# Node passes that hold loaded and stored tiles twice and load a turn ahead

## What is computed

```python
h = jnp.maximum(_layernorm(x, axis=-1), 0.0)
x = x + _L0_gnn_ref(h, edge_attr_8, ...)            # message passing, product with W_upd
h = jnp.maximum(_layernorm(x, axis=-1), 0.0)
x = x + _L1_gnn_ref(h, edge_index, edge_attr_8, ...) # convolution by edge attributes
h = jnp.maximum(_layernorm(x, axis=-1), 0.0)
x = x + _L2_gnn_ref(h, edge_attr_8, src, dst, ...)   # encoder, 2 rounds of edge and node MLP, decoder
h = jnp.maximum(_layernorm(x, axis=-1), 0.0)
x = x + _L3_gnn_ref(h, edge_index, edge_weight, ...) # 2 GCN convolutions
```

## Time and profile before

| | before |
|---|---|
| median of 3 runs | 24420.91 us (24419.03 to 24428.73) |
| profiled execution | 24420.0 us |
| its span | 24418.2 us |
| busy PE, DVE, ACT, POOL | 78%, 55%, 25%, 23% of the span |
| node passes: first reduction to last store, n0 to n6 | 160, 367, 347, 329, 348, 91, 73 us |
| one turn's compute, n0 to n6 | 19.4, 59.4, 60.7, 53.2 to 54.5, 58.1 to 59.6, 11.8, 6.3 us |

### The profile page before, as it was taken

The page is one execution under the profiler, slowest core; times in us unless marked ns, Lnnn a source line. Parts: engine busy times, 40 slices in busy tenths (PEclk is TensorE's granted clock), DMA queues, the critical chain, the costliest instruction groups (busy, mean ns, idle before and its releaser), DMA issues. The chain is left out here.

```text
span 24418.2 us, 718381 instructions
## 1 busy us (share of the span) xinstructions
PE 18952.0 (78%) x285234; PEld 16845.7 (69%) x285234; DVE 13480.2 (55%) x32301; ACT 6107.4 (25%) x12086; POOL 5619.6 (23%) x3991
## 2 busy tenths in 40 slices
PE   0566666666569996799999999959999999769797
PEld 0555555555549996678777778747777777668797
DVE  1777777777644444444444444444444444456565
ACT  0111111111112221344444444422222222211111
POOL 0788888888700000000000000000000000001010
PEclk9655555555557776899999999979999999855555
DMA  2222222222212221233333333324444444334444
GB/s 83 45 50 48 49 48 49 51 49 48 47 55 88 90 88 56 87 101 100 100 100 100 100 100 100 100 65 128 130 129 128 130 129 129 100 95 151 120 153 129
DMA packets 1485401, 2230.06 MB, mean 91 GB/s; under 512 B 773860, under 2 KB 961010, under 8 KB 1440840
## 3 DMA queue, kind: packets, MB, share of 16 engines
q1 hardware_dynamic: 1168296, 1839.20, 24.1%
q10 hardware_dynamic: 176604, 300.32, 3.3%
q0 software_dynamic: 139040, 67.50, 2.9%
HBM read 1651.47 MB, written 551.16 MB: 90 GB/s over the span
## 5 line engine op out<-in xcount | busy, mean ns | idle before, releaser
L751 POOL DMA_INDIRECT records<-e_sort_rec,e_sort_index x3300 | 4775.9, 1447 | 1063.5 <-issue 1058.0
L2193 PE MATMUL e_s_ps_g<-e_s_parts,e_s_pick 128*128 128x64 bf16 x65340 | 3040.3, 203 | 717.5 <-DVE e_s_to_hot L1877 303.2
L2193 PEld LDWEIGHTS e_s_ps_g<-e_s_parts,e_s_pick 128*128 128x128 bf16 x65340 | 2777.4, 105 | 860.6 <-issue 374.5
L2286 POOL DMA_INDIRECT e_s_spill<-send,e_s_lists x220 | 212.8, 967 | 11482.2 <-DVE e_s_g_sb L1897 5895.5
L1893 DVE COPY e_s_g_sb<-e_s_ps_g 128x512 f32<-128x512 f32 x880 | 607.4, 690 | 2656.4 <-PE e_s_ps_h L2216 1251.2
L1317 PE MATMUL e_s_g<-e_s_parts,e_s_pick 128*128 128x16 bf16 x65340 | 1782.9, 174 | 319.6 <-DVE e_s_values L1233 219.8
L2198 PE MATMUL e_s_ps_g<-e_s_window,e_s_to_hot 128*128 128x64 bf16 x23100 | 2015.9, 202 | 3.7 <-issue 3.7
L1317 PEld LDWEIGHTS e_s_g<-e_s_parts,e_s_pick 128*128 128x128 bf16 x65340 | 1761.7, 104 | 348.5 <-DVE e_s_values L1233 240.3
L2240 PE MATMUL e_s_ps_sum<-e_s_unit,e_s_wide 128*128 128x128 f32 (+1 forms) x15400 | 1914.8, 276 | 5.3 <-DVE e_s_merged L1957 5.2
L1074 PE MATMUL e_sort_acc<-e_sort_thirds,e_sort_hot 128*128 128x48 f32 x7260 | 1574.6, 414 | 364.0 <-DVE e_sort_hot L912 364.0
L1074 PEld LDWEIGHTS e_sort_acc<-e_sort_thirds,e_sort_hot 128*128 128x128 f32 x7260 | 1557.0, 332 | 396.4 <-DVE e_sort_hot L912 396.4
(11 more groups left out here) (481 smaller groups left out, 33848.1 us busy)
## 6 DMA issues: line engine op xcount, KB each, us to landing
e_s_rows<-rows_d SPq DMA_DIRECT2D x330, 1088.0 KB, 5.3
e_s_hot<-hots_d SPq DMA_DIRECT2D x550, 560.0 KB, 3.6
e_s_states<-states SPq DMA_DIRECT2D x880, 256.0 KB, 4.2
e_s_to_rows<-rows_d SPq DMA_DIRECT2D x220, 608.0 KB, 6.1
e_s_rows<-rows_d SPq DMA_DIRECT2D x220, 544.0 KB, 4.9
e_s_rows<-rows_d SPq DMA_DIRECT2D x220, 512.0 KB, 3.9
e_s_to_rows<-rows_d SPq DMA_DIRECT2D x220, 512.0 KB, 4.9
states<-e_s_first_t ACTq DMA_DIRECT2D x440, 256.0 KB, 2.1
```

The source lines that it names most:

```text
L751: pool.indirect_dma_start(records, bass.IndirectOffsetOnAxis(ap=index[x][:, t:t + 1], axis=0), rec[x][:, t, :], None,).then_inc(written[x] ...
L2193: pe.matmul(to_, pick[p][:, h, here], parts[:, SPAN * c + h, r, :], start=h == 0 and r == 0, stop=False)
```

## The change

Tiles that are loaded or stored, and the table tile, are allocated twice; turn i uses the copy of its parity (`bigs[i % 2]`, `turns[i % 2]`). The other tiles stay single. SP issues the loads and the tables of turn i+1 ahead of the stores of turn i. Before load(i) with i at least 2 it waits for the end of the chains of turn i-2 and for the stores up to turn i-2, and for every i above 0 it waits until the loads of turn i-1 have landed. Since the loads no longer wait for the end of the turn before, DVE does: before turn i it waits for the end of all five chains of turn i-1. The memset clears both table tiles, and SP waits for both. The five turns are written out on all engines in place of one and a loop, so counts and addresses are constants, and the increments of `sp_tick` are gone. The bodies of the steps are the same; they take the tiles as an argument.

```diff
@@ node_pass @@
             if step == steps[0]:
-                return node_loaded, i * (16 * n_loads) + (b_loaded + 16 * n_loads)
+                return node_loaded, (i + 1) * (16 * n_loads) + b_loaded
...
-                sp.wait_ge(tables_cleared[name], 1)
+                sp.wait_ge(tables_cleared[name], 2)
...
-                    sp.dma_start(big["tab"][:, :, k, :], node_rows(agg[k])[bass.ds(i, 1)].squeeze(0)).then_inc(node_loaded, 16)
+                    sp.dma_start(bigs[i % 2]["tab"][:, :, k, :], node_rows(agg[k])[i]).then_inc(node_loaded, 16)
...
-                load_tables(0)
-
-            def body(i, first, last=False):
-                if not first:
+            def load(i):
+                if i >= 2:
                     for u in range(K):
-                        sp.wait_ge(q[u].sem, q[u].end(i - 1))
-                        sp.sem_inc(sp_tick, 1)
-                    sp.wait_ge(node_stored, i * (16 * len(stores)) + b_stored)
-                    sp.sem_inc(sp_tick, 1)
+                        sp.wait_ge(q[u].sem, q[u].end(i - 2))
+                    sp.wait_ge(node_stored, (i - 1) * (16 * len(stores)) + b_stored)
+                if i:
+                    sp.wait_ge(node_loaded, i * (16 * n_loads) + b_loaded)
                 for tile, rows_ in loads:
-                    sp.dma_start(tile, node_rows(rows_)[bass.ds(i, 1)].squeeze(0)).then_inc(node_loaded, 16)
-                if tables is not None and not last:
-                    for u in range(K):
-                        sp.wait_ge(q[u].sem, q[u].at("agg_sum", i))
-                        sp.sem_inc(sp_tick, 1)
-                    load_tables(i + 1)
+                    sp.dma_start(by_unit(bigs[i % 2][tile]), node_rows(rows_)[i]).then_inc(node_loaded, 16)
+                if tables is not None:
+                    load_tables(i)
+
+            load(0)
+            for i in range(NODE_TURNS):
+                if i + 1 < NODE_TURNS:
+                    load(i + 1)
                 for rows_, tile, step in stores:
                     for u in range(K):
                         sp.wait_ge(q[u].sem, q[u].at(step, i))
-                        sp.sem_inc(sp_tick, 1)
-                    sp.dma_start(node_rows(rows_)[bass.ds(i, 1)].squeeze(0), by_unit(big[tile])).then_inc(node_stored, 16)
-
-            body(0, True)
-            with sp.Fori(1, NODE_TURNS - 1) as i:
-                body(i, False)
-            body(NODE_TURNS - 1, False, True)
+                    sp.dma_start(node_rows(rows_)[i], by_unit(bigs[i % 2][tile])).then_inc(node_stored, 16)
             sp.wait_ge(node_stored, b_stored + 16 * len(stores) * NODE_TURNS)
...
-                dve.memset(big["tab"][:, :, :, :], 0.0).then_inc(tables_cleared[name], 1)
-            rolled(dve, NODE_TURNS, lambda i, first: dve_body(dve, q, ready, i))
+                for x in range(2):
+                    dve.memset(bigs[x]["tab"][:, :, :, :], 0.0).then_inc(tables_cleared[name], 1)
+            for i in range(NODE_TURNS):
+                if i:
+                    for u in range(K):
+                        dve.wait_ge(q[u].sem, q[u].end(i - 1))
+                dve_body(dve, q, ready, i, t=turns[i % 2])
...
-                rolled(act, NODE_TURNS, lambda i, first: act_body(act, q, ready, i))
+                for i in range(NODE_TURNS):
+                    act_body(act, q, ready, i, t=turns[i % 2])
...
-                rolled(pe, NODE_TURNS, lambda i, first: pe_body(pe, q, ready, i))
+                for i in range(NODE_TURNS):
+                    pe_body(pe, q, ready, i, t=turns[i % 2])
@@ pass_scope @@
-    def pass_scope(name, tiles):
+    def pass_scope(name, tiles, twice):
...
-        big = {k: sb(f"{name}_{k}", [shape[0], K] + shape[1:], F32, st) for k, shape in tiles.items()}
-        t = {k: [tile[:, u] for u in range(K)] for k, tile in big.items()}
+        big = [{k: sb(f"{name}_{k}", [shape[0], K] + shape[1:], F32, st) for k, shape in tiles.items()}]
+        big.append({k: sb(f"{name}_{k}_odd", [shape[0], K] + shape[1:], F32, st) if k in twice else big[0][k] for k, shape in tiles.items()})
+        t = [{k: [tile[:, u] for u in range(K)] for k, tile in big[x].items()} for x in range(2)]
```

More of the change, by code:

```diff
@@ L2727, in edge_pass, with node_pass @@
             advance(scattered[t], 16 * UNITS)
-    def node_pass(name, loads, tables, stores, steps, dve_body, act_body, pe_body, bufs, big):
+    def node_pass(name, loads, tables, stores, steps, dve_body, act_body, pe_body, bufs, bigs, turns):
         q = [Chain(node_chain[u], base(node_chain[u]), steps) for u in range(K)]
@@ L2919, in _gnn, with n0_dve, n0_act @@
     st, t, ps, big = pass_scope("n0", dict(x=[P, C, F], c=[P, C, F], sq=[P, C, F], v=[P, 3, 8], h=[P, C, F], ht=[TW, P],
-                                      y=[P, 512]))
+                                      y=[P, 512]), ("x", "h", "y"))
     with st:
-        def n0_dve(dve, q, ready, i, t=t):
+        def n0_dve(dve, q, ready, i, t):
             ln_relu(dve, q, ready, "x", i, t["x"], t["c"], t["sq"], t["v"], t["h"])
-        def n0_act(act, q, ready, i, t=t, ps=ps):
+        def n0_act(act, q, ready, i, t, ps=ps):
             for u in range(K):
@@ L2931, in n0_act, with n0_pe @@
                 act.activation(t["y"][u], ps[u][0:P, :], ACT.Copy).then_inc(q[u].sem, 1)
-        def n0_pe(pe, q, ready, i, t=t, ps=ps):
+        def n0_pe(pe, q, ready, i, t, ps=ps):
             for u in range(K):
@@ L2951, in _gnn, with n1_dve @@
                                       x1=[P, C, F], c=[P, C, F], sq=[P, C, F], v=[P, 3, 8], h=[P, C, F], ht=[TW, P],
-                                      y=[P, 512]))
+                                      y=[P, 512]), ("x", "h0", "x1", "h", "y", "tab"))
     with st:
-        def n1_dve(dve, q, ready, i, t=t, ps=ps):
+        def n1_dve(dve, q, ready, i, t, ps=ps):
             for u in range(K):
@@ L2977, in n1_dve, with n1_act @@
             ln_relu(dve, q, ready, "x", i, t["x1"], t["c"], t["sq"], t["v"], t["h"])
-        def n1_act(act, q, ready, i, t=t, ps=ps):
+        def n1_act(act, q, ready, i, t, ps=ps):
             for u in range(K):
@@ L3000, in n1_act, with n1_pe @@
                 act.activation(t["y"][u], ps[u][0:P, :], ACT.Copy).then_inc(q[u].sem, 1)
-        def n1_pe(pe, q, ready, i, t=t, ps=ps):
+        def n1_pe(pe, q, ready, i, t, ps=ps):
             for u in range(K):
@@ L3098, in n2_dve, with n2_act @@
             ln_affine(dve, q, ready, "enc", i, ps, t["sqd"], t["v"], "nenc", t["n"])
-        def n2_act(act, q, ready, i, t=t, ps=ps):
+        def n2_act(act, q, ready, i, t, ps=ps):
             for u in range(K):
@@ L3110, in n2_act, with n2_pe @@
             send_recv_act(act, q, ready, i, t, ps)
-        def n2_pe(pe, q, ready, i, t=t, ps=ps):
+        def n2_pe(pe, q, ready, i, t, ps=ps):
             for u in range(K):
@@ L3125, in n2_pe @@
             send_recv_pe(pe, q, ready, i, t, ps, 0, "n")
-        node_pass("n2", [(by_unit(big["x"]), x1_d)], (agg1, 1),
+        node_pass("n2", [("x", x1_d)], (agg1, 1),
                   [(x2_d, "x2", "x_new"), (dis_d, "dis", "dis"),
@@ L3180, in _gnn, with n3_dve, n3_act, n3_pe @@
                       a=[2 * D, 2 * P], sqd=[P, C, D], v=[P, 3, 8], n=[P, C, D], nt=[2 * D, 2 * P])
-    st, t, ps, big = pass_scope("n3", node_tiles | dict(send=[P, C, D], recv=[P, C, D]))
+    st, t, ps, big = pass_scope("n3", node_tiles | dict(send=[P, C, D], recv=[P, C, D]), ("prev", "n", "send", "recv", "tab"))
     with st:
-        def n3_dve(dve, q, ready, i, t=t, ps=ps):
+        def n3_dve(dve, q, ready, i, t, ps=ps):
             node_update_dve(dve, q, ready, i, t, ps, 0)
-        def n3_act(act, q, ready, i, t=t, ps=ps):
+        def n3_act(act, q, ready, i, t, ps=ps):
             node_update_act(act, q, ready, i, t, ps, 0)
             send_recv_act(act, q, ready, i, t, ps)
-        def n3_pe(pe, q, ready, i, t=t, ps=ps):
+        def n3_pe(pe, q, ready, i, t, ps=ps):
             node_update_pe(pe, q, ready, i, t, ps, 0)
             send_recv_pe(pe, q, ready, i, t, ps, 1, "n")
-        node_pass("n3", [(by_unit(big["prev"]), n0_d)], (agg2, 1),
+        node_pass("n3", [("prev", n0_d)], (agg2, 1),
                   [(n1_d, "n", "node_new"),
@@ L3242, in n4_pe @@
                 by_node(pe, ps[u], t["a2"][u], w_dec1[:, :], F).then_inc(q[u].sem, 1)
[L3244 to L3245 removed]
+        node_pass("n4", [("prev", n1_d), ("x", x2_d),
+                         ("dis", dis_d)], (agg2, 2),
                   [(x3_d, "x3", "x_new"), (g1_d, "g", "h_dis")],
                   node_update + ["node_turned", "node_t", "dec_hidden", "dec_act", "dec", "dec_bias", "x_new"]
[L3248 removed]
+                  + ln_names("x", False) + ["h_dis"], n4_dve, n4_act, n4_pe, st, big, t)
     edge_pass("e4", [(g1_d, F, "src")], "dst", F, agg3, "gcn")
@@ L3262, in _gnn, with n5_dve @@
     st, t, ps, big = pass_scope("n5", dict(tab=[P, S, TW], s=[P, C, F], g=[P, C, F], dis=[P, C], sT=[TW, P], a=[2 * TW, P],
```

(22 more changed lines are left out.)

24 lines of the change are left out of this document (12 added, 12 removed).

## The result

The changed kernel takes 24163.6 us (median of 4 runs, 24155.4 to 24174.6) against 24423.1 us before, ratio 0.9893 with a 95% interval of 0.9881 to 0.9905. The forecast was 24092.5 us with a range of 24045 to 24145. The result is 71 us above it: 260 us were gained where 328 were forecast. The profiled execution, from which all that follows is read, took 24174.6 us.

What follows compares the result with a forecast made beforehand. Node passes were taken as bound by a strict row of compute, store, wait, load, wait. 24420.0 - 323.9 (gaps) - 29.8 (n6) + 19.6 (memset) + 2.4 (DVE wait) + 4.2 (code) = 24092.5 us, range 24045 to 24145.

Steps and rivals of the forecast that it cites:

- rival (b): Written-out turns in the node passes: fresh code costs 32 us, 28 us more than forecast, about 24120 us; chance 10%.
- edge passes of another length: Sign against the forecast: sorted edge passes between the node passes change in time; given no size.
- Gaps of n0 to n5: First six node passes: all idle gaps between turns vanish because loads run a turn ahead, 323.9 us less.
- The new wait of DVE: Turn boundaries in node passes: DVE waits for all five chains' end, 0.1 us at each of 24, 2.4 us more.
- n6: Last node pass: turns too short to hide the loads, so only 29.8 of its 41.1 us of gaps go.
- microsecond in n6: Last node pass: stores queued behind the next load on SP; taken at nothing, a microsecond if the cover goes.
- Second memset: Start of each node pass with tables: clearing a second table tile is exposed, six clears cost 19.6 us more.
- Written-out code: Node passes: turns 2, 3 and 4 also meet fresh code, 21 more turns at 0.2 us, 4.2 us more.
- Transfers beside compute: Node passes: DMA transfers now run while engines compute; claimed to be free.
- rival (a): Fourth and fifth node passes: PE's granted clock rises when gaps go, 37 us less, some 24055 us; chance 10%.
- (c): Node passes: loads do not run ahead, all gaps stay and table loads join them, 24548 us; chance 3%.
- (d): Node passes: gaps only partly hidden as tables and stores contend, 20 to 60 us less gain, 24112 to 24150; chance 10%.

Runs made afterwards that it cites:

- e2: Not a run: the third sorted edge pass, between node passes; 6197 us in the kernel before, 6306 us in the changed kernel.
- e3: Not a run: the fourth sorted edge pass, between node passes; 4836 us in the kernel before, 4779 us in the changed kernel.
- e5: Not a run: the sixth and last sorted edge pass, between node passes; 1293 us in the kernel before, 1305 us in the changed kernel.
- e0: Not a run: the first sorted edge pass, between node passes; 6095 us in the kernel before, 6098 us in the changed kernel.
- e1: Not a run: the second sorted edge pass, between node passes; 2388 us in the kernel before, 2392 us in the changed kernel.
- e4: Not a run: the fifth sorted edge pass, between node passes; 1306 us in the kernel before, 1306 us in the changed kernel.

## Why the prediction was wrong

**The step that failed** is not a term of the sum but one that is missing from it. "The diff touches the node passes alone" was taken to mean that the rest keeps its time. I asked of the written-out turns only what they cost where they stand ("21 more" turns of fresh code, 4.2 us, rival (b) 32 us) and not what they push along behind them. The edge passes gave back 70 us: e2 +109, e3 -58, e5 +11, the rest +8. e2 and e3 are shown to come from the place of PE's code. Of e5's 11 us some 7 follow the written-out turns too (1331 and 1334 us in the two kernels with rolled turns at the slower level, 1337 to 1341 in the four with written-out ones; 1293 against 1300 to 1305 at the faster level). They do not seem to go by PE's place, since the written-out kernels of the faster level have four different places and PE's jumps in e5 take 11 us in sum in all of them, as before; what it is stays open, as do the other 8 us. I had named "edge passes of another length" as what would make me wrong, and gave it neither a chance nor a price. Since the two effects have opposite signs, the range should have been wider on both sides: at place 60 for e3, where it is, but with e2 at one of the other places tried, the same change would have taken an estimated 24174.6 - 109 = 24065 us in the profiled execution, inside the range.

**Point by point.**
- Gaps of n0 to n5 (323.9 us to go): right. All are gone, n5's too; nothing in n0 to n5 waits for a load after turn 0.
- The new wait of DVE (2.4 us): 24 x 0.23 = 5.5 us. SP's hand-over stayed at 0.1 us (461.83 to 461.92 in n0), but DVE's takes 0.23; that its five waits make the difference is likely and not shown.
- n6 (29.8 of 41.1 us): 25.9. The load of turn 2 took the 8.6 us I had taken, the later ones 9.1 and 8.7. The store of turn 1 was due at 24137.4 and issued at 24138.06, because load(2) was in front of it; this is the "microsecond in n6" that I took at nothing. The larger part is the store itself, taken at 3.2 us from its issue to the next load: those of turns 0 to 2 took 4.1, 5.2 and 5.9 us, with a load in front of them.
- Second memset (19.6 us): 24.2, by the 1.55 us pause in n3 and n4 and 0.35 us in the others. I had allowed for an error only downwards. Waiting for it later gave back 20 to 25 us.
- Written-out code (4.2 us): nothing in n0, 5 x 19.40 us where turn 1 had 19.61 before. Rival (b) falls.
- Transfers beside compute at nothing: right. n0 computes 19.40 us a turn at a DMA share of 0.25, where the earlier trace rows had 0.04.
- The clock, rival (a): it did not rise. The windows over the turns of n4:

```profile
21177.53:21238.80 61.27, 32.48 (x140) 26.80 (x140) 36.97 (x195) 12.13 (x30) 0.00 (x0) 0.61 0.14 40
...
21300.52:21358.71 58.19, 29.38 (x140) 24.73 (x140) 36.98 (x195) 12.13 (x30) 0.00 (x0) 0.68 0.15 42
```

  Turns with a granted clock of 0.61 take 61.3 us, turns with 0.68 take 58.2. n4 computes 6.3 us longer in all than before, n3 2 us longer, n2 5.5 us shorter, all within the 12 us I had allowed; in the second trace of the changed kernel n4 is 3.8 us shorter, so much of that is chance. The section "Loop structure matters more than you think" of the Trainium skill's "TensorE: Matmul & The Clock Gate" warns that waits for DMA in a loop bring the clock down. Here the waits went, and the clock did not rise: n4's turns had 0.64 to 0.68 before and have 0.61 to 0.68 now.
- (c) and (d) did not happen.

The node passes came out 11.5 us above my sum, and 70.6 us came from outside it: together the 82 us by which the profiled execution, at 24174.6 us, lies above the forecast. The median is 11 us below that execution, so it is 71 us off.

## What to carry to other kernels

Where loops are long on an engine, code added ahead of them changes their time: price a change that grows or shrinks the code by what it moves, and after the run compare the stretches that the diff does not touch, one by one, before explaining the sum. If "issue" is what ends the idle time ahead of the first instruction of a loop's body, try a few dozen idle instructions ahead of the loop, at several counts; here 60 were worth 0.2%, and 134 cost 0.3%. And a wait that is raised from one event to two belongs at the first use of the second.

## What the runs showed of the hardware

- PE's jump back to the head of a loop of 2447 and 2901 instructions took between 0.36 and 3.6 us by the loop's place, the same again after moving it by 256; in loops of 1667 and fewer it took 0.2 us at every place tried.
- Each of the 596 jumps longer than 0.5 us ended 1.34 to 1.57 us after a packet of 16384 bytes of the instruction queue had landed. The loops of 2447 and 2901 instructions had 10 to 13 such packets in nearly every pass, the loops of 1667 and fewer none.
- A short jump does not mean a short pass: e3 had its shortest time, 4775 to 4780 us, at place 60, and 4805 to 4827 at 134 and 200 with jumps as cheap. What the places do inside the loop was not taken apart.
- DVE paused for 1.55 us between two memsets of 7680 elements a partition and 0.35 us between two of 1920, with nothing to wait for that the profile shows.
- 122 semaphore instructions on PE, each with a wait that is met and an increment, took 18.6 us, 0.15 us each.
- The same kernel ran at two levels 193 to 197 us apart. The difference lies in e0, e1, e4 and e5; e2 and e3 differ by at most 20 us. What sets the level was not tried.
